# A decoder layer on one core: x in four loads with its norm first, and the context's products in three passes

## The chip, the cores and the metric

The kernel runs on one core of a Trainium2 chip. The metric is device time in microseconds (us); the time before is the median of three runs. The engines are called as the profile calls them: PE is TensorE (PEld its weight loads), ACT is ScalarE, DVE is VectorE, POOL is GpSimd, and SP is the engine that issues the DMAs here.

## The reference

x is 4 sequences of 256 tokens of width 256 (1024 tokens); the context is 4 x 256 tokens of width 128. Cut to what matters:

```python
x = x + attn(layernorm(x), Wq, Wk, Wv, Wb, bb, Wg, Wo, convs...)   # 16 heads, gated linear recurrence
x = x + xattn(layernorm(x), ctx, cWq, cbq, cWk, cbk)               # teacher_logits = layernorm(x)
x = x + ffn(layernorm(x), router, 16 routed + 1 shared expert)     # top 4 of 16

def xattn(y, ctx, Wq, bq, Wk, bk):
    query = einsum('bnc,dc->bnd', ctx, Wq) + bq
    key   = einsum('bnc,dc->bnd', ctx, Wk) + bk
    attention = softmax(einsum('bnd,bmd->bnm', query, key))
    return einsum('bln,bmn->blm', y, attention)
```

`query` and `key` depend on the context alone, so they can be computed at any time before the attention; the kernel does so at its start.

## The kernel before, in words

One program holds the whole layer; every engine has its own hand-written order of instructions, and semaphores tie them together. N = 512 tokens is a chunk (`c`, two of them); P = 128 features or tokens is a tile (`t`, eight token tiles); KT = 2 halves of the width 256 (`kt`).

Most products are made in three passes (`mm3`, lines 1344 to 1348): each operand is split into a high part in fp32r and a low part (the rest), and the passes are hi*lo, lo*hi and hi*hi. ACT writes the high part of a weight (`high`, L613), POOL the low part (`split_low`, L444). A plain fp32 `mm` (L1342) is one instruction in the program; the trace records two MATMULs for it.

The start of the program, which the change rewrites, runs like this:

- SP issues the loads in one queue: x in two halves (L298), the context's weights `xw`, the context `ctxT` and the bias `xb` (L299 to L301), `ident`, `wb`, `bb`, then head 0's weights, its parameters and values, head 1's weights and parameters. The next, `load_weights(0, 2)`, waits for head 0's low part.
- DVE writes two zero buffers (L989, L990), takes statistics of x per token tile (L971), computes `rstd` and `nmr` in a chain of small instructions (`norm_factors`, L926 to L966), and normalises token tiles 2, 3, 6 and 7 (`half_norm`, L977). ACT normalises tiles 0, 1, 4 and 5 (L585).
- PE multiplies the context with its weights (`context_qk(u)`, u = 0 to 3, into banks 4 to 7), transposes the normalised x (`half_transpose`, L1357, 8 transposes for each chunk; chunk 0 needs tiles 0 to 3), and ACT drains both: `context_out` (L600) and `half_out` (L593). `half_out` writes the high part of xT, and DVE writes its low part (`half_low`, L986).
- Then PE makes head 0: `project_in(0, 0, what, chunks)` for q (what = 0), k (1) and the gate (2), 6 matmuls for each chunk; between q and k come `beta_logits` (12 matmuls) and after k `beta_tokens` (8 small transposes). Each q or k chunk is drained from one of two banks by `first_taps` on ACT (L637, L639), the next two taps of the convolution are DVE's (`taps`, L1070), and the last is POOL's (`last_tap`, L459). `project_in` for the gate waits until DVE has finished the taps of the chunk that used the same bank.
- The sigmoid of beta (L716, with a table load ahead of it) is on ACT, between `first_taps` of q and `first_taps` of k. From it DVE makes the decay rows (`obetT`, L1112 and L1114), which go to memory and come back as a broadcast.

The order on ACT before the change, from the first instruction on: the split of `wb`, `high(0, 0)`, the split of the values' weights, `context_out(0)`, `context_out(1)`, the four tiles of `half_norm`, `context_out(2)`, the four `half_out`, `context_out(3)`, `high(0, 1)`, `first_taps(0, 0, (0, 1))`, two sigmoids, `first_taps(0, 0, (2, 3))`, the gates. The order on PE: `context_qk(0)`, `(1)`, `(2)`, the 16 transposes, `context_qk(3)`, q's two chunks, `beta_logits`, k's two chunks, `beta_tokens`, the gate's two chunks, head 1's q.

After the start, 16 heads follow in a steady order, then the cross attention, the router and 18 expert blocks.

## Time and profile before

| | us |
|---|---|
| median of three runs | 582.71 |
| the three runs | 580.95, 582.71, 583.91 |
| the profiled execution: its own time | 582.77 |
| the profiled execution: its span | 581.0 |
| PE busy | 556.8 (96%) |
| DVE busy | 433.4 (75%) |
| ACT busy | 398.3 (69%) |
| POOL busy | 292.8 (50%) |

The span runs from the first to the last instruction; the run's own time is 1.8 us longer. PE's 96% counts matmuls that overlap, so it isn't PE at its peak. The granted clock of PE is 0.991 over the whole span. The change touches only what happens in about the first 30 us.

### The profile page before, as it was taken

How to read it: one execution, taken by the hardware profiler on the slowest of the kernel's cores; microseconds unless marked ns; L12 is line 12 of the kernel's file. 1: busy time of each engine (PE TensorE's matmuls, PEld its weight loads, DVE VectorE, ACT ScalarE, POOL GpSimd, SP SyncE). 2: the span in 40 equal slices, each digit the busy share in tenths (PEclk: the TensorE clock that was granted, in tenths of full speed). 3: DMA queues.
4: the chain of work that ended last, by engine and by line, in shares of the span. 5: the costliest groups of instructions: out<-in, count | busy, mean ns of one | idle time of the engine just before them, and what ended most of it. 6: DMA issues, size and time to landing. Idle time of an engine off the chain costs nothing.

```text
span 581.0 us, 9944 instructions
## 1 busy us (share of the span) xinstructions
PE 556.8 (96%) x3392; PEld 487.5 (84%) x3392; DVE 433.4 (75%) x1046; ACT 398.3 (69%) x782; POOL 292.8 (50%) x194
## 2 busy tenths in 40 slices
PE   3898999999999999999999999989799999999997
PEld 1687889989989899899899898877678888888887
DVE  7768998998998899889989988977867543323333
ACT  3978888879778789798797887785653333333431
POOL 2335656656567467466565674420201565556552
PEclk9998999999999999999999999999799999999999
DMA  6032032031030230230211202210100532343221
GB/s 208 23 120 83 0 120 83 1 118 61 24 119 12 72 119 2 82 105 16 83 57 63 83 1 101 82 30 2 55 1 0 168 126 82 111 128 126 86 88 72
DMA packets 18001, 42.31 MB, mean 73 GB/s; under 512 B 4736, under 2 KB 6528, under 8 KB 17952
## 3 DMA queue, kind: packets, MB, share of 16 engines
q1 hardware_dynamic: 17952, 41.69, 21.4%
q8 instruction: 27, 0.44, 0.3%
q14 instruction: 22, 0.18, 0.1%
HBM read 40.47 MB, written 1.21 MB: 72 GB/s over the span
## 4 chain that ended last, share of the span: by engine, by line
PE 88%; ACT 4%; DVE 4%; issue 1%; DMA 1%; SPq 0%; DVEq 0%; ACTq 0%
PE bank L1346 21%; PE bank L1348 20%; PE bank L1347 20%; PE bank L1342 16%; PE bank L1483 5%; PE bank L1471 4%; ACT tok L671 2%; DMA xbias<-in_xb 1%; DVE stats L1051 1%; PE bank L1357 1%; PE bank L1550 1%; ACT values L585 1%; DVE x L1336 0%; DVE raw L1070 0%; DVE xT_lo L986 0%
## 5 line engine op out<-in xcount | busy, mean ns | idle before, releaser
L1346 PE MATMUL bank<-xT_lo,w_hi 128*128 128x512 f32 x320 | 133.7, 418 | 1.9 <-DVE conv L1070 1.2
L1348 PE MATMUL bank<-xT_hi,w_hi 128*128 128x512 f32 x320 | 126.1, 394 | 0.0
L1347 PE MATMUL bank<-xT_hi,w_lo 128*128 128x512 f32 x320 | 125.6, 392 | 0.0
L464 POOL TENSOR_TENSOR gated_lo<-gated,gated_hi 128x512 fp32r<-128x512 f32 x30 | 38.7, 1291 | 116.4 <-ACT gated_hi L691 112.7
L671 ACT ACTIVATE tok<-bank,nmr,rstd 128x128 f32<-128x128 f32 x256 | 91.3, 504 | 2.0 <-DVE nmr L966 2.0
L1346 PEld LDWEIGHTS bank<-xT_lo,w_hi 128*128 128x128 f32 x320 | 60.5, 189 | 16.1 <-DVE conv L1070 3.2
L459 POOL TENSOR_TENSOR conv<-tap,conv 128x506 f32<-128x506 f32 x32 | 61.9, 1935 | 21.7 <-DVE conv L1070 21.7
L459 POOL TENSOR_TENSOR raw<-tap,raw 128x506 f32<-128x506 f32 x32 | 61.9, 1936 | 20.3 <-DVE raw L1070 16.3
L1348 PEld LDWEIGHTS bank<-xT_hi,w_hi 128*128 128x128 f32 x320 | 60.3, 189 | 13.5
L1051 DVE BATCH_NORM_STATS2 stats<-bank 128x6 f32<-128x128 f32 x256 | 56.3, 282 | 16.3 <-PE bank L1471 16.3
L1347 PEld LDWEIGHTS bank<-xT_hi,w_lo 128*128 128x128 f32 x320 | 60.7, 190 | 9.1
L1042 DVE TENSOR_TENSOR_SCAN decay<-obet,dmask 128x1536 f32<-128x1536 f32 x16 | 62.0, 3872 | 0.0
L1226 DVE TENSOR_TENSOR conv<-bank,tok 128x512 f32<-128x512 f32 x36 | 24.9, 690 | 43.8 <-PE bank L1348 43.6
L546 POOL TENSOR_TENSOR gate<-conv,tap 128x512 f32<-128x512 f32 x32 | 42.7, 1340 | 20.5 <-DVE conv L1226 13.2
L1234 DVE TENSOR_TENSOR gated_lo<-gate,gated_hi 128x512 fp32r<-128x512 f32 x32 | 23.6, 775 | 38.9 <-ACT gated_hi L849 38.6
L683 ACT ACTIVATE qk<-bank,prm 128x512 f32<-128x512 f32 x64 | 51.4, 841 | 0.0
L1070 DVE SCALAR_TENSOR_TENSOR raw<-bank,prm,raw 128x510 f32<-128x510 f32 x64 | 46.7, 741 | 5.6 <-ACT tap L639 4.5
L849 ACT ACTIVATE gated_hi<-gate 128x512 fp32r<-128x512 f32 x32 | 18.8, 626 | 46.7 <-PE bank L1348 43.0
L1342 PE MATMUL bank<-qk 128*128 128x256 f32 (+1 forms) x256 | 50.1, 329 | 0.5 <-DVE x L1103 0.3
L1070 DVE SCALAR_TENSOR_TENSOR conv<-bank,prm,conv 128x510 f32<-128x510 f32 x64 | 46.7, 742 | 3.4 <-ACT tap L639 2.2
L1342 PEld LDWEIGHTS bank<-qk 128*128 128x128 f32 x256 | 43.3, 190 | 5.6 <-issue 0.7
L1342 PE MATMUL bank<-probs,values 128*128 128x256 f32 (+1 forms) x256 | 47.0, 327 | 0.0
(184 smaller groups left out, 1403.6 us busy)
## 6 DMA issues: line engine op xcount, KB each, us to landing
obet<-obet_rows SPq DMA_DIRECT2D x16, 768.0 KB, 4.4
w_raw<-in_w SPq DMA_DIRECT2D x22, 384.0 KB, 4.6
tap<-route_rows SPq DMA_DIRECT2D x16, 512.0 KB, 3.9
w_raw<-in_w SPq DMA_DIRECT2D x12, 256.0 KB, 2.9
wv_raw<-in_wv SPq DMA_DIRECT2D x8, 256.0 KB, 4.9
wo_raw<-in_wo SPq DMA_DIRECT2D x8, 256.0 KB, 5.0
w_raw<-in_w SPq DMA_DIRECT2D x12, 128.0 KB, 2.1
x<-in_x SPq DMA_DIRECT2D x2, 512.0 KB, 4.7
```

The source lines that it names most:

```text
L459: nc.gpsimd.tensor_tensor(y, r, y, ALU.add).then_inc(conv_done, 1)
L464: nc.gpsimd.tensor_tensor(gated_lo[:, cc], gated[:, c * N:(c + 1) * N], gated_hi[:, cc].bitcast(F32), ALU.subtract).then_inc(gated_lo_read ...
L546: nc.gpsimd.tensor_tensor(weighted(m, c), prod[:, two(m, c)], wbc[:, s * T + c * N:s * T + (c + 1) * N], ALU.mult).then_inc(e_weighted, 1)
L671: ins = nc.scalar.activation(tok[:, t * P:(t + 1) * P], t_ring[u][:, i * P:(i + 1) * P], ACT.Identity, scale=rstd[:, t:t + 1], bias=nmr[:, ...
L683: nc.scalar.activation(qk[:, u * N:(u + 1) * N], t_ring[u][:, :], ACT.Identity, scale=prm[:, o:o + 1], bias=prm[:, o + 1:o + 2]).then_inc( ...
L1042: nc.vector.tensor_tensor_scan(decay[:, :], obet[:, :], dmask[:, :], 0.0, ALU.mult, ALU.add).then_inc(decay_ready, 1)
L1051: ins = nc.vector.bn_stats(stats[:, 6 * t:6 * t + 6], t_ring[u][:, i * P:(i + 1) * P])
L1070: ins = nc.vector.scalar_tensor_tensor(out=y, in0=r, scalar=prm[:, o + 3 - back:o + 4 - back], in1=y, op0=ALU.mult, op1=ALU.add)
L1342: return nc.tensor.matmul(o, l, r, start=start, stop=stop)
L1346: nc.tensor.matmul(o, l_hi, r_lo, start=start, stop=False, skip_group_check=loose)
L1347: nc.tensor.matmul(o, l_lo, r_hi, start=False, stop=False, skip_group_check=loose)
L1348: return nc.tensor.matmul(o, l_hi, r_hi, start=False, stop=stop, skip_group_check=loose)
```

## The change

- x comes in four loads of 512 columns in place of two of 1024, and the statistics of two token tiles wait for each.
- `xw`, `ctxT` and `xb` are issued by ACT, not by SP.
- The context's four products are made in three passes over high and low parts. ACT writes the high parts of `xw` (128x256) and of `ctxT` (128x1024) before `high(0, 0)`; POOL writes the low parts.
- The two zero buffers are written by POOL, not DVE. POOL's `split_low(0, 0)` waits until DVE has normalised its tiles, where it waited for `rstd`.
- ACT's order: the two high parts, `high(0, 0)`, `half_norm`, `half_out`, the values' weights, `wb`, `first_taps(0, 0, (0,))`, `context_out(0)` and `(1)`, `first_taps(0, 0, (1,))`, `context_out(2)` and `(3)`, `high(0, 1)`, then the sigmoids.
- PE's order: the 16 transposes, `context_qk(0)` and `(1)`, q's two chunks, `context_qk(2)` and `(3)`, `beta_logits` and so on.
- DVE copies `ident` into `dmask` after `half_low` and `wb`'s low part, not before.

```diff
-            for c in range(NCH):
-                sp.dma_start(x[:, c * T:(c + 1) * T], x_in[:, c * T:(c + 1) * T]).then_inc(ld_x[c], 16)
-            sp.dma_start(xw, xw_in).then_inc(ld["ctx"], 16)
-            sp.dma_start(ctxT, ctx_in).then_inc(ld["ctx"], 16)
-            sp.dma_start(xb[:, :], xb_in).then_inc(ld["ctx"], 16)
+            for u in range(TT // 2):
+                sp.dma_start(x[:, u * N:(u + 1) * N], x_in[:, u * N:(u + 1) * N]).then_inc(ld_x[u], 16)
...
-            pool.wait_ge(ln_rstd, NCH)
+            nc.gpsimd.memset(dmask[:, :], 0.0).then_inc(zeros_ready, 1)
+            nc.gpsimd.memset(obetT, 0.0).then_inc(zeros_ready, 1)
+            pool.wait_ge(ctx_hi_ready, 2)
+            nc.gpsimd.tensor_tensor(xw_lo, xw, xw_hi.bitcast(F32), ALU.subtract).then_inc(ctx_lo_ready, 1)
+            nc.gpsimd.tensor_tensor(ctx_lo, ctxT, ctx_hi.bitcast(F32), ALU.subtract).then_inc(ctx_lo_ready, 1)
+
+            pool.wait_ge(ln_norm_dve, 2 * NCH)
             split_low(0, 0)
             low_values(0, 0)
             split_low(0, 1)
...
-            act.wait_ge(ld["beta"], 32)
-            nc.scalar.activation(wb_hi, wb, ACT.Copy).then_inc(small_split, 1)
+            act.dma_start(xw, xw_in).then_inc(ld["ctx"], 16)
+            act.dma_start(ctxT, ctx_in).then_inc(ld["ctx"], 16)
+            act.dma_start(xb[:, :], xb_in).then_inc(ld["ctx"], 16)
...
+            act.wait_ge(ld["ctx"], 48)
+            nc.scalar.activation(xw_hi, xw, ACT.Copy).then_inc(ctx_hi_ready, 1)
+            nc.scalar.activation(ctx_hi, ctxT, ACT.Copy).then_inc(ctx_hi_ready, 1)
             high(0, 0)
+            for c in range(NCH):
+                half_norm(0, c)
+            for c in range(NCH):
+                half_out(0, c, xT_hi)
             act.wait_ge(ld_wv[0], 16)
             nc.scalar.activation(wv_hi[:, 0:N], wv_raw[:, 0:N], ACT.Copy).then_inc(wv_hi_ready, 1)
+            act.wait_ge(ld["beta"], 32)
+            nc.scalar.activation(wb_hi, wb, ACT.Copy).then_inc(small_split, 1)
+            first_taps(0, 0, (0,))
             context_out(0)
             context_out(1)
-            for c in range(NCH):
-                half_norm(0, c)
+            first_taps(0, 0, (1,))
             context_out(2)
-            for c in range(NCH):
-                half_out(0, c, xT_hi)
             context_out(3)
             high(0, 1)
-            first_taps(0, 0, (0, 1))
...
-            obet_zero = steps.did(nc.vector.memset(obetT, 0.0))
-            a = steps.did(nc.vector.memset(dmask[:, :], 0.0))
-
             for t in range(TT):
-                dve.wait_ge(ld_x[t // G], 16)
+                dve.wait_ge(ld_x[t // 2], 16)
                 ins = x_stats(t)
...
-                pe.wait_ge(ld["ctx"], 48)
+                pe.wait_ge(ctx_lo_ready, 2)
                 s, c = divmod(u, NCH)
-                mm(bank[4 + u][:, :], xw[:, s * P:(s + 1) * P], ctxT[:, c * N:(c + 1) * N],
-                   True, True).then_inc(x_qk_full, 1)
-
+                w, t = slice(s * P, (s + 1) * P), slice(c * N, (c + 1) * N)
+                mm3(bank[4 + u][:, :], xw_hi[:, w], xw_lo[:, w], ctx_hi[:, t], ctx_lo[:, t],
+                    True, True).then_inc(x_qk_full, 1)
+
+            pe.wait_ge(ld["const"], 16)
+            for c in range(NCH):
+                half_transpose(0, c)
             context_qk(0)
             context_qk(1)
-            pe.wait_ge(ld["const"], 16)
-            context_qk(2)
-            for c in range(NCH):
-                half_transpose(0, c)
-            context_qk(3)
...
             project_in(0, 0, 0, (1,))
+            context_qk(2)
+            context_qk(3)
             beta_logits()
```

## Rows read from the trace of the kernel before

**Rows 1.** The head of the profile's page.
```profile
span 581.0 us, 9944 instructions
```

**Rows 2.** The chain that ended last, in order of time: start us, us, what.
```profile
2.70 5.92 DMA xbias<-in_xb
8.66 3.79 PE bank L1342 x4
12.48 0.69 ACT attT L600
13.17 1.97 ACT values L585 x4
...
18.07 0.23 PE bank L1347
...
47.70 0.43 PE bank L1346
```

**Rows 3.** Timeline of PE: start us, us, engine, line, operation, tiles [idle before <-releaser].
```profile
8.66 4.86 PE L1342 MATMUL bank<-raw 128*128 128x512 f32 x6 [8.66 <-DMA xbias<-in_xb]
14.20 2.08 PE L1357 MATMUL bank<-ident,values 128*128 128x128 f32 x16 [0.68 <-ACT values L585]
16.12 1.02 PE L1342 MATMUL bank<-raw 128*128 128x512 f32 x2
17.57 0.50 PE L1346 MATMUL bank<-xT_lo,w_hi 128*128 128x512 f32 x1 [0.42 <-DVE xT_lo L986]
...
27.83 0.50 PE L1346 MATMUL bank<-xT_lo,w_hi 128*128 128x512 f32 x1 [1.19 <-DVE conv L1070]
```

**Rows 4.** Timeline of ACT, first 27 us.
```profile
9.81 0.84 ACT L613 ACTIVATE w_hi<-w_raw 128x768 fp32r<-128x768 f32 x1 [0.42 <-DMA w_raw<-in_w]
10.56 0.62 ACT L702 ACTIVATE wv_hi<-wv_raw 128x512 fp32r<-128x512 f32 x1
...
13.07 2.07 ACT L585 ACTIVATE values<-x,nmr,rstd 128x256 f32<-128x256 f32 x4
...
17.51 0.71 ACT L600 ACTIVATE attT<-bank,xbias 128x512 f32<-128x512 f32 x1
18.09 0.87 ACT L613 ACTIVATE w_hi<-w_raw 128x768 fp32r<-128x768 f32 x1
19.33 0.78 ACT L637 ACTIVATE conv<-bank,prm 128x512 f32<-128x512 f32 x1 [0.37 <-PE bank L1348]
...
22.00 1.28 ACT L716 ACT_TABLE_LOAD   x1
...
24.79 0.78 ACT L637 ACTIVATE conv<-bank,prm 128x512 f32<-128x512 f32 x1 [0.25 <-PE bank L1348]
```

**Rows 5.** Timeline of DVE, first 26 us.
```profile
6.55 1.40 DVE L971 BATCH_NORM_STATS2 stats<-x 128x6 f32<-128x256 f32 x4 [0.30 <-DMA x<-in_x]
...
10.49 3.87 DVE L977 TENSOR_SCALAR values<-x,rstd,nmr 128x256 f32<-128x256 f32 x4
...
24.58 1.09 DVE L1112 TENSOR_SCALAR gate<-gate 16x1020 f32<-16x1020 f32 x1 [0.80 <-ACT gate L716]
```

**Rows 6.** The instructions of line 977 in the whole trace.
```profile
L977 DVE TENSOR_SCALAR values<-x,rstd,nmr x12: 400/411/1943, 10.5 to 425.6; 128x256 f32<-128x256 f32 x12
```

**Rows 7.** Timeline of POOL.
```profile
10.80 1.81 POOL L444 TENSOR_TENSOR w_lo<-w_raw,w_hi 128x768 fp32r<-128x768 f32 x1 [10.36 <-ACT w_hi L613]
12.56 1.32 POOL L450 TENSOR_TENSOR wv_lo<-wv_raw,wv_hi 128x512 fp32r<-128x512 f32 x1
```

**Rows 8.** Busy time by stretch: PE, PEld, DVE, ACT, POOL, granted clock, DMA share, GB/s.
```profile
5.00:10.00 5.00, 1.34 (x2) 0.82 (x3) 4.40 (x20) 0.42 (x2) 0.00 (x0) 1.00 1.00 341
```

**Rows 9.** Stretches of another view of that kind, later in the span.
```profile
47.00:48.00 1.00, 1.00 (x6) 0.90 (x5) 1.00 (x3) 1.00 (x5) 1.00 (x2) 0.50 0.00 0
...
410.00:415.00 5.00, 2.60 (x13) 1.97 (x11) 4.80 (x15) 3.19 (x6) 3.58 (x2) 0.71 0.33 87
```

**Rows 10.** Timeline of PE in the cross attention's norm.
```profile
412.05 1.94 PE L1357 MATMUL bank<-ident,values 128*128 128x128 f32 x8 [1.71 <-ACT values L585]
```

More of the change, by code:

```diff
@@ L183, in decoder_layer @@
         xw = raw[:, T:T + 2 * P]
+        ctx_hi, ctx_lo = gated_hi[:, 2 * T:3 * T], gated_lo[:, 2 * T:3 * T]
+        xw_hi, xw_lo = gated_hi[:, 3 * T:3 * T + 2 * P], gated_lo[:, 3 * T:3 * T + 2 * P]
         qctx, kctx = attT[:, 0:T], attT[:, T:2 * T]
@@ L253, in decoder_layer @@
               ("const", "tie", "ctx", "beta", "router", "obet", "wo", "obet_rows", "route_rows", "out")}
-        ld_x = [sem(f"ld_x{i}") for i in range(NCH)]
+        ld_x = [sem(f"ld_x{i}") for i in range(TT // 2)]
         ld_w = [sem(f"ld_w{i}") for i in range(2)]
@@ L283, in decoder_layer @@
         obet_ready, dmask_ready = sem("obet_ready"), sem("dmask_ready")
+        zeros_ready = sem("zeros_ready")
+        ctx_hi_ready, ctx_lo_ready = sem("ctx_hi_ready"), sem("ctx_lo_ready")
         r_full, r_score = sem("r_full"), sem("r_score")
@@ L998, in _ @@
                 half_norm(0, c)
+            for c in range(NCH):
+                half_low(0, c)
+            dve.wait_ge(small_split, 1)
+            nc.vector.tensor_tensor(wb_lo, wb, wb_hi.bitcast(F32), ALU.subtract).then_inc(b_lo_ready, 1)
             dve.wait_ge(ld["const"], 16)
-            steps.after(a)
+            dve.wait_ge(zeros_ready, 1)
             dm = dmask[:, :].rearrange("p (b c) -> p b c", b=B)
@@ L1006, in _ @@
             ins.then_inc(dmask_ready, 1)
-            for c in range(NCH):
-                half_low(0, c)
-            dve.wait_ge(small_split, 1)
-            nc.vector.tensor_tensor(wb_lo, wb, wb_hi.bitcast(F32), ALU.subtract).then_inc(b_lo_ready, 1)
             def context_max(e):
@@ L1108, in _ @@
             dve.wait_ge(b_ready, NCH)
-            steps.after(obet_zero)
+            dve.wait_ge(zeros_ready, 2)
             bt = betaT.rearrange("h (b t) -> h b t", b=B)
@@ L1362, in context_qk @@
             def context_qk(u):
-                pe.wait_ge(ld["ctx"], 48)
+                pe.wait_ge(ctx_lo_ready, 2)
                 s, c = divmod(u, NCH)
-                mm(bank[4 + u][:, :], xw[:, s * P:(s + 1) * P], ctxT[:, c * N:(c + 1) * N],
-                   True, True).then_inc(x_qk_full, 1)
+                w, t = slice(s * P, (s + 1) * P), slice(c * N, (c + 1) * N)
+                mm3(bank[4 + u][:, :], xw_hi[:, w], xw_lo[:, w], ctx_hi[:, t], ctx_lo[:, t],
+                    True, True).then_inc(x_qk_full, 1)
+            pe.wait_ge(ld["const"], 16)
+            for c in range(NCH):
+                half_transpose(0, c)
             context_qk(0)
             context_qk(1)
-            pe.wait_ge(ld["const"], 16)
-            context_qk(2)
-            for c in range(NCH):
-                half_transpose(0, c)
-            context_qk(3)
             def energies(b):
```

## The prediction, as it was put on record

> **What bounds the kernel now.** I began with the page's head (a span of 581.0 us [rows 1]) and the chain that ended last. Through the heads that chain is nearly all PE, so only a delay or gain at the start that reaches PE's queue counts, and it then counts once. The start of the chain is in [rows 2]: the context's loads land at 8.62, PE makes four records of context products in 3.79 us, ACT drains the second product at 12.48, and only then, at 13.07, does ACT normalise x. The timeline of PE [rows 3] has the rest: 16 transposes from 14.20, the first matmul of q at 17.57, and, the point everything behind hangs on, the first matmul of the gate at 27.83. PE idled 1.19 us before it, for DVE's taps of k.
>
> The timeline of ACT [rows 4] tells what held those taps. From the first drain of q (19.33) to the first drain of k (24.79) ACT is busy but for 0.25 us of waiting. So the start is bounded in two pieces: by the way to the first finished chunk of q, which I call S (19.33 before), and from there by ACT's list of work, not by PE. From 24.79 it is 3.04 us to 27.83 (drain, taps, hand over). After 27.83 the same instructions follow in the same order in both kernels, so I carry the shift of that point to the end one to one.
>
> **Way to S, part by part.**
>
> *Loads.* The statistics of the last half begin at 6.55 and take 1.40 for four tiles [rows 5]; with four loads only two tiles are left behind the last one, 0.70. From the end of the statistics (7.95) to the first norm (10.49) it is 2.54 [rows 5]. No row shows a DMA issued by ACT. The two bounds: the context's 655 KB (1280 columns of 128 partitions) stay behind x and the last x is there at 6.55; or they come in beside x and take 655/341 = 1.9 us from it, 8.45 [rows 8]. In that stretch the 16 DMA engines have a share of 1.00, so bytes that come sooner push others back; I take 8.45. Then the factors are ready at 8.45 + 0.70 + 2.54 = 11.7 (low end 9.8). The low end gains little: `high(0, 0)` stands ahead of the norm on ACT and waits for weights until 9.81, + 0.84 = 10.65 [rows 4]. Those weights stand behind the same bytes as before.
>
> The Trainium skill speaks to this (DMA: Bandwidth & Descriptors, Issuing engines are not separate DMA queues): DMAs of all issuing engines share the 16 engines and interleave, and issuing from another engine saves only the sequencer's time. By that rule the load of x is later, not sooner, which is the value taken above; by the other bound the result would be 0.9 us better.
>
> *ACT before the norm.* The high parts of 256 and 1024 columns: 768 cost 0.84 and 512 cost 0.62 [rows 4], so 0.22 for each 256: 0.40 + 1.06 = 1.5 us. They lie between the context's landing (8.62 at the latest, as before) and 10.1, beside ACT's wait for head 0's weights; they cost at most 0.3. The table load stands behind ACT's three issues and is hidden under the same wait. The zero buffers go from DVE, which was waiting for x, to POOL, which was idle until 10.80; no row has a POOL memset, and even at the rate of POOL's subtraction (1.32 for 512 columns [rows 7]) 1536 columns take 4 us and are done before POOL has other work: nothing either way.
>
> *DVE's norm against POOL.* One norm tile takes 0.41 in the median and 1.94 at worst [rows 6]; the four of the start took 3.87 together, and they lay beside POOL's subtractions at 10.80 and 12.56 [rows 5, 7]. So DVE is held while POOL subtracts. The new wait removes `split_low(0, 0)` from that place, but the context's low parts are put there: 768 columns take 1.81 and 512 take 1.32, so 0.8 + 2.3 = 3.1 us from about 9 or 10 to 12 or 13. DVE's two tiles for chunk 0 are done somewhere between 11.3 and 13. ACT's two are done at 11.7 + 2 x 0.52 = 12.75. I let the transposes begin at T0 = 12.7 (bounds 11.8 and 13.2), 1.5 earlier than before. `split_low(0, 0)` then ends at about 15.3, ahead of its use; `low_values` and `split_low(0, 1)` have until past 28.
>
> *PE's pace.* This is where I see the change lose. Before, PE began at 8.66 with the context, and those records were slow: four in 3.79 us, against two in 1.02 later [rows 2, 3], so 0.95 against 0.51 each, and the granted clock column doesn't show it [rows 8]. That slow time lay in front of the norm, where PE had nothing else; when the transposes came they ran at 2.08 for 16. Now PE is idle until T0, and the transposes are its first work. Half pace at other places has a matmul at 0.43 against 0.23 [rows 2], with the granted clock at 0.50 (1.2 of 2.4 GHz) [rows 9], and eight transposes in 1.94, 0.24 each [rows 10], with the clock falling in that stretch. The slow start before lasted from 8.66 to about 12.7. I let it last as long again: from T0 to 16.7, just the transposes: 16 x 0.24 = 3.9, end 16.6. Then two context products of three passes at 0.23: 1.4. q begins at 18.0 (17.57 before), and S is 1.76 later as before: 19.8.
>
> The Trainium skill has a rule here that would make it worse (TensorE: Matmul & The Clock Gate, Part 4: PE-mode transpose): transposes don't count as activity that opens the clock. By it the half pace would go on behind them; the second rival below prices that from rows.
>
> **From S to the gate.** Before, ACT needed 24.79 - 19.33 - 0.25 = 5.2 us. Now four `context_out` stand in the list (17.51 to 18.09 is 0.58 for one [rows 4]): 2.3. `high(0, 1)`, which ran ahead of S at 18.09, stands there too: 0.83. That is 8.35, so k's first drain is at 28.1, 3.3 later. PE is not late for it: q's second chunk, two context products (1.4), `beta_logits` (2.8) and k's first chunk end some 7 us after S. POOL: `split_low(0, 1)` (1.8) now begins with `high(0, 1)`'s end, and two `last_tap` of 1.3 follow back to back, beside DVE's 1.09 us instruction on beta [rows 5], of the kind that POOL holds: about 0.5 more. The gate then begins at 28.1 + 3.04 + 0.5 = 31.7, which is 3.9 later. What SP has behind the beta rows (head 0's decay broadcast, parameters and weights of later heads) is late by the same 4 us, and so is its use.
>
> The sum, on the profiled run's own time of 582.77: 582.8 + 3.9 = 586.7. That run lies within 0.1 us of the median of the runs shown, so the number stands for the median too.
>
> What the change removes is true work for PE (eight fp32 records, for which twelve passes come: 8 x 0.51 against 12 x 0.23, a gain of 1.3), but PE isn't what binds from S to the gate, so I count that as hidden by the wait.
>
> **Rivals.**
>
> *PE is at full pace.* If the slow records before were not a slow clock but something of the fp32 form or of the operands' arrival (for it: the clock column shows 1.00; against it: the same form ran at 0.51 later), the transposes take 2.1 and, from T0 = 11.8, q begins at 15.3: 2.7 better than the sum, +1.2. With T0 = 12.7 it is +2.1. So 583.9 to 584.9, not slower by what a measurement can tell. It decides from a half-pace stretch under about 2 us on.
>
> *The half pace lasts longer.* It goes on through the two context products (+1.4) and q's first chunk (+1.3 more): 588.1 to 589.4. For it: around 412.05, where PE had mostly transposes, the clock didn't stay up [rows 9, 10]. Against it: the only start that the trace has was over in 4 us.
>
> *The clock falls in the new gap.* Between k's second chunk and the gate PE has 3 us with only eight small transposes in them; before, it idled 1.19 there [rows 3] and the next matmuls were at full pace. If it falls as it has by 47 [rows 9], the gate's first six or seven matmuls go at 0.43 for 0.23 and the transposes with them: +1.7, 588.4.
>
> *Faster after all.* For 0.5% the gate would have to come 2.9 us sooner than before, so S before 12; the weights' landing at 9.81 alone forbids it, unless head 0's weights land several us sooner. It is left with a residue.
>
> **How the numbers follow.** The measurement of this kernel tells about 0.5% (2.9 us) from no change, so slower begins at 585.6. Forecast as summed, 585.6 to 588: 0.45. Full pace or a start between it and the sum, 583.5 to 585.6: 0.31. Longer half pace: 0.13. Clock falls in the gap: 0.06. Faster or far outside: 0.05. Slower is 0.45 + 0.13 + 0.06 less a little for a median that comes low, 0.62; same 0.33; faster 0.05. The range takes in both neighbours: 583.2 (full pace, T0 at its lower bound, the 0.5 of POOL left away) to 589.2 (half pace through both).
>
> **What would show it.** Right: the transposes begin at 12 to 13 and take near 4 us; q begins near 18; ACT's drain of k's first chunk near 28 with no wait ahead of it; the gate's first matmul near 31.7, PE idle 2 to 3 us before it; from there on the same distances as before. x's last statistics would begin near 8.4. Wrong: transposes at 0.13 each from the start; or an ACT that waits for PE ahead of k's drain, which would mean that PE, not ACT's list, binds there; or the distance from the gate to the end shorter than 553 us, which would mean that the later heads had slack for a late start or that the clock fell less often. If x lands at 6.55 in spite of the context's loads, the term for the loads is wrong by 0.9 us.

## The result and the profile after

The changed kernel takes 592.34 us in the median of four runs (591.82 to 592.63). The kernel before took 582.07 beside it (580.95 to 583.91), so the ratio is 1.0171, with a 95% interval of 1.0146 to 1.0196: slower by 1.7%, 10 us. I had put 586.7 on record, with a range that ended at 589.2. The direction was right, the size was not. Of the 10.3 us between the medians 9.05 lie between the two profiled executions; the rest is that the one of the kernel before (582.77) was 0.7 above its median and the one of the changed kernel (591.82) 0.5 below.

The profiled execution has a span of 590.0 us, 9.0 more than before. First the timeline of PE in it, to be held against [rows 3] (start, duration, engine, line, operation, tiles, idle time ahead of it and what ended that):

```profile
15.91 3.65 PE L1369 MATMUL bank<-ident,values 128*128 128x128 f32 x16 [15.91 <-ACT values L591]
19.21 0.78 PE L1358 MATMUL bank<-gated_lo,gated_hi 128*128 128x512 f32 x1
...
21.57 0.39 PE L1358 MATMUL bank<-xT_lo,w_hi 128*128 128x512 f32 x1
...
35.43 0.80 PE L1358 MATMUL bank<-xT_lo,w_hi 128*128 128x512 f32 x1 [3.27 <-DVE conv L1082]
36.02 0.63 PE L1359 MATMUL bank<-xT_hi,w_lo 128*128 128x512 f32 x1
...
41.57 0.42 PE L1360 MATMUL bank<-xT_hi,w_hi 128*128 128x512 f32 x1
```

The transposes begin at 15.91, 1.7 us later than before, although nothing stands ahead of them on PE now. q begins at 21.57 (17.57 before), the gate at 35.43 (27.83 before), and behind the gate the matmuls run at half pace up to 41.6. The chain that ended last has their spacing:

```profile
20.84 0.42 PE bank L1358
21.27 0.23 PE bank L1359
...
36.22 0.43 PE bank L1359
...
41.34 0.41 PE bank L1359
41.76 0.23 PE bank L1360
```

The busy time by stretch gives the granted clock (the column ahead of the last two): 0.50 of full speed, 1.2 GHz, from 35 to 40.

```profile
35.00:40.00 5.00, 4.57 (x11) 3.61 (x12) 1.98 (x4) 0.80 (x2) 2.52 (x2) 0.50 0.55 178
```

The timeline of DVE, against [rows 5]:

```profile
8.08 1.50 DVE L985 BATCH_NORM_STATS2 stats<-x 128x6 f32<-128x256 f32 x4
...
9.82 0.66 DVE L943 SCALAR_TENSOR_TENSOR nw<-nw 128x8 f32<-128x8 f32 x1
10.41 0.16 DVE L946 TENSOR_TENSOR nw<-stats 128x8 f32<-128x8 f32 x1
10.52 2.28 DVE L948 SCALAR_TENSOR_TENSOR nw<-nw 128x8 f32<-128x8 f32 x1
...
14.72 1.38 DVE L991 TENSOR_SCALAR values<-x,rstd,nmr 128x256 f32<-128x256 f32 x4
...
31.47 1.08 DVE L1124 TENSOR_SCALAR gate<-gate 16x1020 f32<-16x1020 f32 x1 [2.85 <-ACT gate L730]
32.47 1.46 DVE L1126 TENSOR_SCALAR gate<-gate 16x508 f32<-16x508 f32 x1
```

and that of POOL, against [rows 7]:

```profile
9.70 0.76 POOL L477 TENSOR_TENSOR gated_lo<-raw,gated_hi 128x256 fp32r<-128x256 f32 x1 [6.28 <-ACT gated_hi L710]
10.42 2.35 POOL L478 TENSOR_TENSOR gated_lo<-raw,gated_hi 128x1024 fp32r<-128x1024 f32 x1
...
28.95 1.84 POOL L445 TENSOR_TENSOR w_lo<-w_raw,w_hi 128x768 fp32r<-128x768 f32 x1 [6.86 <-ACT w_hi L621]
30.75 2.91 POOL L460 TENSOR_TENSOR conv<-tap,conv 128x506 f32<-128x506 f32 x2
```

Read the two together. The other small instructions of the norm factors (128x8) take 0.16 or 0.17 each, but L943 takes 0.66 and L948 takes 2.28, and both end with a POOL subtraction: 9.70 + 0.76 = 10.46, and 10.42 + 2.35 = 12.77. The same thing meets DVE's second instruction on beta: 1.46 where 0.41 would do, about until POOL's two last taps are done at 33.66. The norm tiles themselves now take 1.38 for four, not 3.87 [rows 5].

The timeline of ACT, against [rows 4]:

```profile
14.72 2.08 ACT L591 ACTIVATE values<-x,nmr,rstd 128x256 f32<-128x256 f32 x4 [3.76 <-DVE nmr L980]
...
23.22 0.78 ACT L645 ACTIVATE conv<-bank,prm 128x512 f32<-128x512 f32 x1 [2.38 <-PE bank L1360]
...
24.47 1.27 ACT L606 ACTIVATE attT<-bank,xbias 128x512 f32<-128x512 f32 x2
...
31.34 0.76 ACT L645 ACTIVATE conv<-bank,prm 128x512 f32<-128x512 f32 x1
```

From q's drain (23.22) to k's (31.34) ACT doesn't wait at all: 8.1 us of its own list, 5.5 before.

**Where the 9.0 us are.** The gate begins 7.6 later. Up to there: the last statistics end at 9.58 (7.95 before), +1.6; the factors take 5.14 to the first norm (2.54), +2.6; ACT's wait from factors to norm is gone (2.58), -2.6; from ACT's norm to the transposes nearly nothing; from the transposes to q 5.66 (3.37), +2.3; q's start to its drain 1.65 (1.76), -0.1; drain to drain 8.12 (5.46), +2.7; k's drain to the gate 4.09 (3.04), +1.05. Together 7.6 (these go by the timeline). From the gate to the last of head 0's next norm factors (L980 at 54.20, L966 at 43.55 before) it is 18.77 (54.20 - 35.43; before 43.55 - 27.83 = 15.72), +3.05. And from there to the end the changed kernel is 1.65 shorter: the half-pace stretch that the kernel before had from 46.9 to 50.3 [rows 2, 9] isn't there.

### The profile page after: what moved, and what is told of

Its sections match the earlier page's. It is cut to its first block, busy times and chain, and to the rows that moved or that the text cites. A ratio compares the mean times of both kernels' runs of the same rounds, so it can differ in the third digit from the quotient of the medians.

```text
span 590.0 us, 9958 instructions
## 1 busy us (share of the span) xinstructions
PE 556.8 (94%) x3396; PEld 490.5 (83%) x3396; DVE 434.1 (74%) x1044; ACT 399.8 (68%) x784; POOL 298.7 (51%) x198
## 4 chain that ended last, share of the span: by engine, by line
PE 86%; DVE 6%; ACT 5%; issue 2%; DMA 1%; SPq 0%; DVEq 0%; ACTq 0%
PE bank L1358 20%; PE bank L1360 20%; PE bank L1359 20%; PE bank L1354 15%; PE bank L1494 5%; PE bank L1482 4%; ACT tok L679 2%; PE bank L1369 1%; DMA x<-in_x 1%; DVE stats L1063 1%; PE bank L1561 1%; DVE x L1348 0%; DVE raw L1082 0%; DVE xT_lo L1000 0%; DVE nw L948 0%
## 5 line engine op out<-in xcount | busy, mean ns | idle before, releaser
L1082 DVE SCALAR_TENSOR_TENSOR raw<-bank,prm,raw 128x510 f32<-128x510 f32 x64 | 46.9, 743 | 8.5 <-ACT tap L647 7.2
L1082 DVE SCALAR_TENSOR_TENSOR conv<-bank,prm,conv 128x510 f32<-128x510 f32 x64 | 46.9, 743 | 3.4 <-ACT tap L647 2.3
```

What stands on the lines that cost most here:

```text
L1082: ins = nc.vector.scalar_tensor_tensor(out=y, in0=r, scalar=prm[:, o + 3 - back:o + 4 - back], in1=y, op0=ALU.mult, op1=ALU.add)
```

## The experiments

All times are medians; each is compared by its ratio to the kernel before, measured beside it on the same chip. That kernel's median was between 580.92 and 582.36 there, so ratios can be compared across the table, and times only to about 1 us. The changed kernel stands at 1.0171. "Transposes begin" is by the timeline (14.20 before). "q" and "gate" are the starts of their first matmuls in the chain that ended last (17.57 and 27.83 before); the chain counts a matmul from the end of the one ahead of it, which makes q 21.73 in the changed kernel where the timeline has 21.57. The runs are told below in another order than in the table.

| | ratio (95%) | us | transposes begin | q | gate |
|---|---|---|---|---|---|
| changed kernel | 1.0171 (1.0146 to 1.0196) | 592.34 | 15.91 | 21.73 | 35.43 |
| context's low parts behind the norm | 1.0139 (1.0121 to 1.0157) | 589.94 | 13.75 | 19.99 | 33.64 |
| all loads on SP | 1.0114 (1.0091 to 1.0136) | 588.62 | 14.84 | 20.61 | 34.28 |
| PE busy ahead of the transposes | 1.0138 (1.0121 to 1.0156) | 589.92 | 17.68 | 21.00 | 34.66 |
| gap ahead of the gate filled | 1.0135 (1.0117 to 1.0152) | 589.63 | 16.00 | 20.89 | 34.56 |
| drains of the context behind k | 1.0125 (1.0111 to 1.0139) | 589.45 | 16.04 | 20.93 | 32.34 |
| one pass | 1.0122 (1.0106 to 1.0137) | 589.31 | 13.64 | 19.77 | 33.47 |
| two loads of x | 1.0155 (1.0130 to 1.0181) | 590.80 | 15.73 | 21.87 | 35.58 |
| four edits together | 1.0102 (1.0082 to 1.0122) | 587.63 | 13.12 | 18.43 | 32.36 |
| and ACT's list cut | 1.0031 (1.0016 to 1.0046) | 582.97 | 13.94 | 18.59 | 29.24 |
| kernel before, four loads | 1.0026 (1.0010 to 1.0043) | 583.84 | 15.28 | 18.64 | 28.93 |
| kernel before, norm first | 0.9951 (0.9934 to 0.9967) | 579.42 | 12.03 | 15.23 | 26.22 |

**POOL holds the norm factors.** The wait for DVE's norm was put ahead of the context's low parts:

```diff
+            pool.wait_ge(ln_norm_dve, 2 * NCH)
             pool.wait_ge(ctx_hi_ready, 2)
             nc.gpsimd.tensor_tensor(xw_lo, xw, xw_hi.bitcast(F32), ALU.subtract).then_inc(ctx_lo_ready, 1)
             nc.gpsimd.tensor_tensor(ctx_lo, ctxT, ctx_hi.bitcast(F32), ALU.subtract).then_inc(ctx_lo_ready, 1)
-
-            pool.wait_ge(ln_norm_dve, 2 * NCH)
```

> The changed kernel with one wait moved on POOL: it makes the context's low parts only when DVE has normalised x. Theory: in the changed kernel DVE's norm factors (two SBUF inputs) are held while POOL subtracts, one for 2.28 us and one for 0.66, in place of 0.17. Then here both take 0.17, ACT's norm begins at about 12.1 in place of 14.72 and the transposes at about 13.3 in place of 15.91. The context's low parts (3.1 us) then end at about 17, so the products of the context begin there and not at once behind the transposes; the low part of head 0's weights comes 1.8 later, at 18.5 to 19. I expect q's first matmul near 19.5 to 20 in place of 21.57, and 590 us in place of 592.3. Rival: the delay of the norm factors has another cause; then ACT's norm stays at 14.7 and the time rises to 594 or more.

The timeline of DVE in this run:

```profile
10.27 0.17 DVE L943 SCALAR_TENSOR_TENSOR nw<-nw 128x8 f32<-128x8 f32 x1
10.35 0.17 DVE L946 TENSOR_TENSOR nw<-stats 128x8 f32<-128x8 f32 x1
10.47 0.17 DVE L948 SCALAR_TENSOR_TENSOR nw<-nw 128x8 f32<-128x8 f32 x1
...
12.56 1.38 DVE L991 TENSOR_SCALAR values<-x,rstd,nmr 128x256 f32<-128x256 f32 x4
```

Both held instructions are back at 0.17 and the transposes begin 2.2 sooner, though x came 0.5 later in this execution. The median is 589.94 for the 590 expected. The run with one pass shows the same from the other side: with no subtraction of the context at all, the transposes begin at 13.64.

**The context's loads beside x.** The three loads went to SP, behind x:

```diff
             for u in range(TT // 2):
                 sp.dma_start(x[:, u * N:(u + 1) * N], x_in[:, u * N:(u + 1) * N]).then_inc(ld_x[u], 16)
+            sp.dma_start(xw, xw_in).then_inc(ld["ctx"], 16)
+            sp.dma_start(ctxT, ctx_in).then_inc(ld["ctx"], 16)
+            sp.dma_start(xb[:, :], xb_in).then_inc(ld["ctx"], 16)
...
-            act.dma_start(xw, xw_in).then_inc(ld["ctx"], 16)
-            act.dma_start(ctxT, ctx_in).then_inc(ld["ctx"], 16)
-            act.dma_start(xb[:, :], xb_in).then_inc(ld["ctx"], 16)
```

> The changed kernel with the context's three loads issued by SP behind x. Theory: the loads on ACT's queue share the DMA engines with x; here the last statistics of x begin at about 6.6 in place of 8.08. The norm factors then begin at about 8.1 in place of 9.6. If the context's high parts stay at 8.3 to 9.7, POOL's subtractions begin when the factors are half done, and ACT's norm begins between 12 and 13.2 in place of 14.72: 590 to 591 us. Rival: the DMAs do not share, x lands at the same time, no change from 592.3.

The median (588.62) is below what was expected, but the profiled execution was the slowest of the four (590.63, the others 587.93 to 589.14), so its places account for only 1.2 us of the gain. And my account of x was off. DVE's timeline:

```profile
3.95 0.75 DVE L984 BATCH_NORM_STATS2 stats<-x 128x6 f32<-128x256 f32 x2 [3.95 <-DMA x<-in_x]
4.98 0.75 DVE L984 BATCH_NORM_STATS2 stats<-x 128x6 f32<-128x256 f32 x2 [0.28 <-DMA x<-in_x]
6.12 0.75 DVE L984 BATCH_NORM_STATS2 stats<-x 128x6 f32<-128x256 f32 x2 [0.39 <-DMA x<-in_x]
8.13 0.75 DVE L984 BATCH_NORM_STATS2 stats<-x 128x6 f32<-128x256 f32 x2 [1.25 <-DMA x<-in_x]
...
11.42 3.92 DVE L990 TENSOR_SCALAR values<-x,rstd,nmr 128x256 f32<-128x256 f32 x4
```

The first three of the four loads come 1.1 to 2.2 us sooner than beside the context, but the statistics of the last still begin at 8.13. What this order gains is that only two tiles stand behind it, and that the context now lands late (ACT's high parts begin at 10.02, against 8.26), so that POOL's subtraction misses the factors and holds the norm tiles in their place (3.92 for four). The expectation had the last load at 6.6; that half of it is wrong.

**Four loads against two.** So I asked the two questions apart: four loads in the kernel before, and two loads in the changed kernel. In the first, only this was changed (with the semaphores that belong to it):

```diff
-            for c in range(NCH):
-                sp.dma_start(x[:, c * T:(c + 1) * T], x_in[:, c * T:(c + 1) * T]).then_inc(ld_x[c], 16)
+            for u in range(TT // 2):
+                sp.dma_start(x[:, u * N:(u + 1) * N], x_in[:, u * N:(u + 1) * N]).then_inc(ld_x[u], 16)
```

> The kernel before with x in four loads and nothing else. In the changed kernel with all loads on SP the last statistics began at 8.13, against 6.55 before, with nothing beside x. Theory: four loads are slower than two, and here too the last two tiles begin at about 8.1; the norm factors end at about 11.3 in place of 10.46, still ahead of ACT's norm at 13.07, so the time stays: 582 to 583. Rival: it was the memory of that day, and the last load is there by 6.6.

The last statistics begin at 7.91 (6.55 before), and everything in the queue behind x is late with them:

```profile
10.88 0.84 ACT L613 ACTIVATE w_hi<-w_raw 128x768 fp32r<-128x768 f32 x1 [0.18 <-DMA w_raw<-in_w]
```

Head 0's weights are there at 10.88 in place of 9.81 [rows 4], the context's products begin at 9.83 in place of 8.66, and q at 18.64 in place of 17.57: the whole start slides by 1.1 us, and the time by 0.26% (0.10 to 0.43). I had expected no change in the time, because I looked at x alone; the loads behind it are what the start hangs on. Another kernel with two loads and the context behind them (the last one below) had its last statistics at 6.59.

This trace shows one thing more. The gate waits 1.19, as in the kernel before, and yet half pace comes, six matmuls later:

```profile
28.93 0.50 PE L1346 MATMUL bank<-xT_lo,w_hi 128*128 128x512 f32 x1 [1.19 <-DVE conv L1070]
...
30.96 0.63 PE L1347 MATMUL bank<-xT_hi,w_lo 128*128 128x512 f32 x1
```

It lasts about eight matmuls, and the later half pace at 47 to 50 isn't there.

The second is the diff the other way round, in the changed kernel.

> The changed kernel with x in two loads again, the context still issued by ACT. In the kernel before, four loads made everything land about 1.1 us later. Theory: here the loads' end comes about 1 us sooner, and with it x and head 0's weights; but the context lands sooner too, so that POOL holds DVE's norm factors as before. ACT's norm begins at 13.5 to 14.2 in place of 14.72: 591 to 592 (592.3 before). Rival: beside the context's loads the form of x's loads doesn't matter, no change.

The last statistics begin at 8.10: beside the context's loads, x's form doesn't matter for x, as the rival said. The ratio fell from 1.0171 to 1.0155, with intervals that overlap, so this run doesn't settle a gain. Against the 6.59 of two loads with the context behind them, it does show what the context's loads beside x cost when x comes in two loads: 1.5 us.

**The slow start of PE.** Six fp32 products of `ident` and x, whose result is overwritten, went ahead of the transposes:

```diff
             pe.wait_ge(ld["const"], 16)
+            pe.wait_ge(ld_x[0], 16)
+            for _ in range(6):
+                mm(bank[7][:, :], ident[:, :], x[:, 0:N], True, True)
             for c in range(NCH):
                 half_transpose(0, c)
```

> The changed kernel with six fp32 products of ident and x in PE's queue ahead of the transposes; their result is overwritten and used nowhere. Theory: the transposes and the first context matmuls are at half pace because PE had done nothing; here the transposes go at 0.12 in place of 0.23 each and the context's at 0.23: q begins about 2.4 us sooner (19.2 in place of 21.57) if the products end by 15.9. Time about 590. Rival: the slow pace belongs to the transposes or to the waits on ACT; then q begins at 21.5 and the time stays at 592.3.

The chain that ended last in this run:

```profile
9.64 8.21 PE bank L1354 x12
17.84 1.75 PE bank L1369 x16
19.59 0.24 PE bank L1358
...
21.00 0.23 PE bank L1358
```

`ident` landed at 9.6 and the products ended at 17.84. ACT's norm began at 15.29 here, and in the changed kernel the transposes follow it by 1.19, so the products held them up by about 1.4. Even so q begins at 21.00, 0.73 sooner than in the changed kernel: 16 transposes take 1.75 for 3.65 and the context's matmuls 0.23 for 0.43. The pace belongs to what PE did before, and not to the transposes. I had expected q 2.4 sooner and about 590 us. The 589.92 was met partly by luck, since the gain in the time (2.4 us) isn't q's alone; in this execution fewer matmuls behind the gate were at half pace, too (about eight, for fourteen, and only from the fifth on), and the granted clock of the stretch from 400 to 440 was 1.00 (0.91 in the changed kernel's).

**The gap ahead of the gate.** Three such products between the beta transposes and the gate:

```diff
             beta_tokens()
+            for _ in range(3):
+                mm(bank[3][:, :], ident[:, :], x[:, 0:N], True, True)
             project_in(0, 0, 2)
```

> The changed kernel with three fp32 products of ident and x (2.6 us) in PE's queue between the beta transposes and the gate, where PE idles 3.27 us; their result is used nowhere. Theory: the clock falls in that gap and the 14 matmuls behind it at 0.43 in place of 0.23 cost 2.8 us. Here the gate begins at 35.4 as before but its matmuls go at 0.23, and the next norm factors come 2.8 us sooner. The half pace that the kernel before the change has at 46.9 to 50.3 may come back further on (1.6 us). Time 589.5 to 591 in place of 592.3. Rival: the clock falls for another reason (the load of the other engines); then no change.

PE's timeline there:

```profile
31.22 2.84 PE L1354 MATMUL bank<-x,ident 128*128 128x512 f32 x6
34.56 0.51 PE L1358 MATMUL bank<-xT_lo,w_hi 128*128 128x512 f32 x1 [0.50 <-DVE conv L1082]
34.90 0.40 PE L1359 MATMUL bank<-xT_hi,w_lo 128*128 128x512 f32 x1
35.14 0.40 PE L1360 MATMUL bank<-xT_hi,w_hi 128*128 128x512 f32 x1
```

Behind the gate the matmuls are 0.23 apart, and the next factors come 15.98 after it (50.54), for 18.77. The half pace comes back further on, at 54.8 to 56.9, as said. 589.63, inside what was expected. About 0.9 of the gain isn't the gap's: the half pace at the start was shorter in this execution, and q began at 20.89 for 21.73.

**ACT's list.** The four drains of the context and `high(0, 1)` were moved behind k's drains:

```diff
-            first_taps(0, 0, (0,))
-            context_out(0)
-            context_out(1)
-            first_taps(0, 0, (1,))
-            context_out(2)
-            context_out(3)
-            high(0, 1)
+            first_taps(0, 0, (0, 1))
...
             first_taps(0, 0, (2, 3))
+            for u in range(2 * NCH):
+                context_out(u)
+            high(0, 1)
             gates(0, 0, range(NCH))
```

> The changed kernel with the four context_out and high(0, 1) moved on ACT behind the drains of k. Theory: these five operations (3.2 us) set when k is drained; without them PE is what k waits for (q's second chunk, the context's last two products, beta), so k's drain begins at about 30.0 in place of 31.34, and DVE's second instruction on beta is no longer held by POOL (1.1 us). The gate begins near 33.1 in place of 35.43, the gap ahead of it is under 2 us and the clock stays up (2.8 us less), while the half pace near 55 comes back (1.6 us more). About 588.8 in place of 592.3. Rival: the start is bound by PE alone, and the gate moves by less than 0.5 us: 592.

k's drain begins at 29.29 behind a wait for PE of 0.74: with the list cut, PE is the bound there. The gate comes at 32.34, 3.1 sooner, with 1.19 of idle time ahead of it, and the clock stays up. But the five operations now hold up the gate's drains (they begin at 36.31), and PE waits 1.6 for them. 589.45, 0.65 more than expected: the list is too long in either place behind q.

POOL is idle here while DVE works on beta, and the first instruction on it is quicker, too:

```profile
28.58 0.68 DVE L1121 TENSOR_SCALAR gate<-gate 16x1020 f32<-16x1020 f32 x1 [1.72 <-ACT gate L724]
```

It took 1.08 in the changed kernel and 1.09 in the kernel before, both times beside a last tap of POOL: it was held in both kernels, the second one only in the changed one.

**The passes themselves.** Plain fp32 for the context, with no high or low part of it; ACT's two splits and POOL's two are gone with the product below, and all the rest of the change stays:

```diff
-                mm3(bank[4 + u][:, :], xw_hi[:, w], xw_lo[:, w], ctx_hi[:, t], ctx_lo[:, t],
-                    True, True).then_inc(x_qk_full, 1)
+                mm(bank[4 + u][:, :], xw[:, w], ctxT[:, t], True, True).then_inc(x_qk_full, 1)
```

> The changed kernel with the context's products as plain fp32, so that ACT makes no high part and POOL no low part of them; everything else of the change stays. Theory: the split costs by POOL's subtractions holding DVE's norm factors (2.6 us); the passes themselves cost nothing. ACT's norm begins at about 12.1, the transposes at 13.2, q near 19 to 20, the gate at 32.5 to 33.5 with the clock falling ahead of it: 589.5 to 590.5, like the run with the low parts behind the norm (589.9). Rival: three passes are what costs, and the time falls near that of the kernel before (582 to 584).

589.31, as expected, and the gate at 33.47 behind 3.17 of idle time. Three passes in place of one are not what costs; of the split, only POOL's subtractions at that moment do.

**Do the parts add up?** Two loads, the low parts behind the norm, three products ahead of the transposes and three ahead of the gate, all as in the diffs above:

> The changed kernel with four of the single edits together: x in two loads, the context's low parts behind the norm, three products ahead of the transposes, three in the gap ahead of the gate. Alone they gave or should give 1, 2.4, 2.4 and 2.7 us; if they add up, 592.3 becomes 583.8. Theory: they don't quite, because the low parts behind the norm are ready only at about 17, so PE waits there for what the quick transposes won: transposes done at 16.1, q at 18.5, k's drain at 28.3 (ACT's list is as long as before), the gate at 32.3 at full pace, and the half pace near 50 comes back. 587.5, give or take 0.8. Rival: they add up, 584.

PE's timeline:

```profile
13.12 2.08 PE L1369 MATMUL bank<-ident,values 128*128 128x128 f32 x16
16.54 0.50 PE L1358 MATMUL bank<-gated_lo,gated_hi 128*128 128x512 f32 x1 [1.34 <-POOL gated_lo L479]
...
18.43 0.47 PE L1358 MATMUL bank<-xT_lo,w_hi 128*128 128x512 f32 x1 [0.23 <-POOL w_lo L445]
```

The quick transposes win time that PE then waits out, for POOL's low parts (1.34) and for head 0's weights (0.23). q begins at 18.43, k's drain at 28.28 and the gate at 32.36 at full pace: 587.63, where the theory said 587.5 and the plain sum 584. In one point the theory didn't hold in the profiled execution (586.04, the quickest of the four): the half pace near 50 did not come back (granted clock 1.00).

That left the gate 4.5 us later than in the kernel before, 3.7 of them between q's start and the gate's, and one candidate for these, ACT's list. In the next kernel it was cut to what it was before the change, with three passes kept (the diff is against the kernel with the four edits):

```diff
-            first_taps(0, 0, (0,))
+            high(0, 1)
             context_out(0)
             context_out(1)
-            first_taps(0, 0, (1,))
-            context_out(2)
-            context_out(3)
-            high(0, 1)
+            first_taps(0, 0, (0, 1))
...
             first_taps(0, 0, (2, 3))
+            context_out(2)
+            context_out(3)
...
-            context_qk(2)
-            context_qk(3)
             beta_logits()
...
             beta_tokens()
-            for _ in range(3):
-                mm(bank[3][:, :], ident[:, :], x[:, 0:N], True, True)
+            context_qk(2)
+            context_qk(3)
```

> The kernel with the four edits together, and ACT's list between the first drain of q and the first drain of k cut to what it was before the change: high(0, 1), context_out(0) and (1) ahead of q's drain, where ACT idles 3.5 us, context_out(2) and (3) behind k's drains; the context's last two products, still in three passes, in the gap ahead of the gate in place of the three idle products. Theory: q begins at 18.4 as there, k's drain at 25.4 to 25.8 in place of 28.28, the gate at 28.5 to 29 in place of 32.36: 583.5 to 584.5 in place of 587.6, the kernel before plus the 0.9 us by which q begins later. Rival: something of the change that isn't yet named costs; the time stays above 586.

ACT's timeline:

```profile
20.32 0.78 ACT L645 ACTIVATE conv<-bank,prm 128x512 f32<-128x512 f32 x1 [1.11 <-PE bank L1359]
...
25.78 0.78 ACT L645 ACTIVATE conv<-bank,prm 128x512 f32<-128x512 f32 x1 [0.25 <-PE bank L1359]
```

From drain to drain it is 5.46, exactly the distance of [rows 4], and the wait for PE is the same 0.25. The gate begins at 29.24, and 582.97 us is 0.31% (0.16 to 0.46) over the kernel before. That is a little under the 583.5 to 584.5 expected, but the kernel before was 1.1 us quicker beside it than beside the changed kernel. So three passes for the context can be had for 0.3%. The other 1.4% went with the five edits together (x in two loads, the low parts behind the norm, PE busy early, the gap filled, the list cut); they weren't priced one by one in this kernel.

**Norm first, with the products left where they warm PE.** The last kernel takes the idea of the change, the norm first, into the kernel before, in plain fp32:

```diff
-            pool.wait_ge(ln_rstd, NCH)
+            pool.wait_ge(ln_norm_dve, 2 * NCH)
             split_low(0, 0)
...
             high(0, 0)
+            for c in range(NCH):
+                half_norm(0, c)
             act.wait_ge(ld_wv[0], 16)
             nc.scalar.activation(wv_hi[:, 0:N], wv_raw[:, 0:N], ACT.Copy).then_inc(wv_hi_ready, 1)
-            context_out(0)
-            context_out(1)
-            for c in range(NCH):
-                half_norm(0, c)
-            context_out(2)
             for c in range(NCH):
                 half_out(0, c, xT_hi)
-            context_out(3)
+            context_out(0)
             high(0, 1)
...
             first_taps(0, 0, (2, 3))
+            context_out(1)
+            context_out(2)
+            context_out(3)
...
             context_qk(0)
             context_qk(1)
             pe.wait_ge(ld["const"], 16)
-            context_qk(2)
             for c in range(NCH):
                 half_transpose(0, c)
-            context_qk(3)
...
             beta_tokens()
+            context_qk(2)
+            context_qk(3)
```

> The kernel before, with plain fp32 products, with the norm first on ACT, POOL's first subtraction behind DVE's norm, two context products ahead of the transposes and two in the gap ahead of the gate, one context_out ahead of q's drain and three behind k's. Theory: PE warms up on the context, the transposes begin at about 12.1, q at 14.4 to 15, k's drain at about 22 in place of 24.79, the gate near 25: 579.5 in place of 582.4, faster than both kernels. Rival: something later binds and the early gain is given back: 582.

ACT's and POOL's timelines:

```profile
10.04 0.84 ACT L613 ACTIVATE w_hi<-w_raw 128x768 fp32r<-128x768 f32 x1 [0.84 <-DMA w_raw<-in_w]
10.79 2.07 ACT L585 ACTIVATE values<-x,nmr,rstd 128x256 f32<-128x256 f32 x4
...
22.45 0.78 ACT L637 ACTIVATE conv<-bank,prm 128x512 f32<-128x512 f32 x1 [0.25 <-PE bank L1348]
```

```profile
11.99 2.69 POOL L444 TENSOR_TENSOR w_lo<-w_raw,w_hi 128x768 fp32r<-128x768 f32 x1 [11.55 <-DVE values L977]
```

The norm begins at 10.79 in place of 13.07, k's drain at 22.45 in place of 24.79, the gate at 26.22. 579.42 us, 0.49% (0.33 to 0.66) faster than the kernel before, and the only one of all that beats it. The time is the 579.5 expected, though the gate came 1.2 later than the 25 expected. q could have begun sooner: PE waited 1.2 for the transposed x, and the chain that ended last goes over ACT's split of the values' weights (L704, 0.5), which stands ahead of the drains of the transposes. The gate could too, since the two fp32 products in the gap end 0.8 after DVE's taps. Neither was tried. POOL's first subtraction took 2.69 for 1.81, beside eight copies of `ident` on DVE (11.83 to 13.00): here it was POOL that was held. It ended at 14.68, ahead of q.

## Why the prediction was wrong

By its own steps, in order:

- *Start of the transposes, 12.7 forecast, 15.91 measured (+3.2).* This is the step that failed most. I had the context's low parts on POOL from 9 or 10 to 12 or 13, had read that DVE is held while POOL subtracts, and put it only on the norm tiles [rows 5, 6, 7], not on the chain of factors that lies in the very same microseconds. It cost 2.6 (5.14 for 2.54), shown by the run with the low parts behind the norm and by the one with one pass. Rather than hold two tiles of DVE beside ACT's norm, it holds everything. The Trainium skill has the rule that I should have looked for (GPSIMD Engine Reference, 1. Specifications): POOL shares its SBUF interfaces with DVE, in contention with DVE instructions of a 2-port mode or with two SBUF inputs. The trace agrees: L948 has two such inputs and took 2.28 for 0.17. The rest is 0.4 from x, since four statistics, not two, stood behind the last landing that DVE waited for, and some 0.2 of hand over.
- *x beside the context, 8.45 forecast, 8.08 measured.* Right in kind and near in size, but partly by luck. I charged 1.9 to the context's loads; with x in two loads they cost 1.5 (8.10 for 6.59). In four loads and with the context behind it, x's last statistics still began at 7.91 and 8.13. What I didn't see is that four loads are slower than two, for all that stands behind them (+1.1 in the kernel before).
- *Transposes at half pace, 3.9 forecast, 3.65 measured.* Right; with PE busy ahead of them they took 1.75.
- *The context's two products, 1.4 forecast, 2.0 measured.* The half pace lasted longer than I let it: 5.4 us from the first transpose, for my 4. The second rival had this as far as 2.7 (by its own rows 2.6, since six matmuls of q at 0.43 for 0.23 are 1.2); 0.6 of it came.
- *From q's drain to k's, 8.35 forecast, 8.12 measured; no wait for PE.* Right, and the run with the list cut back to 5.46 shows that it is this list.
- *POOL beside the beta instruction, 0.5 forecast, 1.05 measured.* Right place, but the first instruction, which I named, was held as long in the kernel before (1.09 and 1.08; 0.68 with POOL idle). The 1.05 more are the second's (1.46 for 0.41).
- *The clock in the gap, left out of the sum, +3.05 measured.* The third rival, to which I gave 6 in 100 and 1.7 us. PE idled 3.27 with eight small transposes ahead, and the 14 matmuls behind it went at 0.43. I had worked out the gap itself (3 us, for 1.2 before) and had rows of half pace at 47 [rows 2, 9]. What stands ahead of them in the trace of the kernel before is two waits with four transposes between:

```profile
45.31 0.66 PE L1483 MATMUL bank<-ident,tok 128*128 128x128 f32 x4 [1.48 <-ACT tok L671]
46.72 0.99 PE L1483 MATMUL bank<-ident,tok 128*128 128x128 f32 x4 [0.74 <-ACT tok L671]
```

To call it unlikely had no row of a gap of 3 us behind it. Filling the gap brought the 15.98, near the 15.72 before. In part the gap only moves the fall: the stretch at 46.9 to 50.3 of the kernel before is gone in the changed kernel (-1.65), though the same two waits are there (1.77 and 0.74, at 55.97 and 57.37), and it came back where the gap was filled.

- *The shift is carried to the end one to one.* Right but for those 1.65.

So 3.9 forecast, + 3.2 for the start of the transposes, + 0.4 from there to q, - 0.3 for both drains, + 0.55 for POOL and the beta, + 3.05 - 1.65 for the clock: 9.1, against 9.0 between the spans. Between the medians it is 10.3, for the reason given with the result. The spread of the kernel before (3 us) goes with the mean granted clock on record with each execution: in the 17 beside the kernel with ACT's list cut it took 582.3 to 582.6 at 0.990 or 0.991, 580.5 to 581.0 at 0.993 to 0.997 and 579.3 or 579.4 at 0.999. The changed kernel's four all had 0.985 to 0.988.

Two sums of the prediction don't come out of its own terms, without touching the forecast: "S before 12" for a gain of 0.5% should be S before 13, and the ends of the range 583.5 and 589.4 for 583.2 and 589.2.

What stays open: how long PE stays at half pace behind its first work differed between executions (5.4 us in the changed kernel, 6.1 with the low parts behind the norm, about 3.5 in the run with the gap filled, whose start is the same program). So does what follows the gap ahead of the gate. In all six executions with a gap of 3.2 or 3.3 us half pace followed, but for 14 matmuls (changed kernel, all loads on SP), 13 (one pass), about 8 (PE busy ahead) or 7 (low parts behind the norm, two loads); in the last three the later half pace (near 50 to 60) came as well, in the first three not. With the gap filled or 1.19 long the gate's matmuls stayed at full pace in every kernel but the one before with four loads. That a long gap brings the fall is shown; what decides how long it lasts, and whether a short one brings it, isn't.

So the single edits' gains of 1.5 to 3.7 us hold some of that play. The intervals of the low parts behind the norm, PE busy ahead, the gap filled and the two loads overlap with that of the changed kernel; those of the loads on SP, the drains behind k and the one pass don't. The places in the traces, not the ratios, carry the argument for each part. The ratios of the two combined kernels and of the norm-first kernel stand clear.

## What to carry to other kernels

When work is moved to POOL, lay its span over DVE's timeline and charge it to every DVE instruction with two SBUF inputs that falls in it, the tiny ones of a dependent chain above all, since a 0.17 us instruction waited out a 2.3 us one here; a `tensor_scalar` from SBUF to SBUF (the norm tiles, beta) was held, too. In this prologue it paid to give PE work first (q came 0.7 sooner, although the work held the transposes up by 1.4), and what is moved behind the first result belongs into a wait that is there in the profile, not into the list that spaces the results. A gap of 3 us ahead of a row of matmuls cost the gap and, for 7 to 14 matmuls, half the pace behind it: price both, and look whether a fall further on goes away for it.

## What the runs showed of the hardware

- A 128x8 `scalar_tensor_tensor` on DVE took 0.17 us alone and 2.28 and 0.66 beside a POOL subtraction, ending with it. A 16x1020 `tensor_scalar` took 0.68 with POOL idle and 1.08 beside a tap of POOL. The other way round, a POOL subtraction of 1.81 took 2.69 beside eight copies on DVE.
- x in four loads of 2 KB a partition landed later than in two of 4 KB: the last statistics began at 7.91 against 6.59, and the weights behind them at 10.88 against 9.81 to 10.04.
- PE's first matmuls went at 0.43 for 512 columns, half pace, while the column of the granted clock said 1.00 (changed kernel, 15 to 25). Where the transposes were all that PE had done, the next matmuls were at 0.23 at once in the runs with the gap filled and with the drains moved (16 transposes in 3.5 us, context at full pace from 19.5). So the transposes did bring the full clock here, against the rule of the Trainium skill that the prediction weighed (TensorE: Matmul & The Clock Gate, Part 4: PE-mode transpose); the measurement decides.
- Half pace behind a wait of PE: after 3.2 or 3.3 us in six of six executions; after 1.19 in one of three (the kernel before with four loads), and there only six matmuls later.
